# Row maxima of an attention in three bank fillings instead of four, with its stages dealt over six slots instead of seven

## The chip, the cores and the metric

The kernel is one program on one core of a Trainium2 chip. The metric is the device time of one execution in microseconds (us). The core has TensorE (PE in the profile, its weight loads PEld), VectorE (DVE), ScalarE (ACT), GpSimd (POOL) and SyncE (SP), which here only issues transfers. Each takes its own instructions in program order; they meet through semaphores. TensorE writes PSUM, eight banks of 128 partitions by 512 fp32 numbers, and VectorE and ScalarE read it out.

## The reference

Two transformer-like layers over x, 8 batches of 112 rows of 256, with a context of 8 batches of 375 rows. The first step is the one that the change touches:

```
x = x + attention_16_heads(layernorm(x), ctx, ctx)     # heads of 16 columns, scores 112 x 375 a head
x = x + mixture_of_8_experts(layernorm(x))             # each token to its best expert, 112 a slot
x = x + attention_1_head(layernorm(x), ctx, ctx, mask)
x = x + ffn_with_low_rank(layernorm(x))

scores = einsum(q, k) / sqrt(16); attn = softmax(scores, over the 375)
out = (attn @ v) @ Wo.T + bo
```

The softmax of the first attention takes each row's true maximum over the 375 context rows off before the exponential.

## The kernel before

The first attention works block by block; a block is a batch of 112 rows with its 16 heads. The heads stand in four groups of four. A head of a group lies on its own 32 partitions, so four matmuls of 32 rows run side by side into banks 0 to 3, one bank a head. Banks 0 and 1 are the LOW pair and 2 and 3 the HIGH pair: each pair has one semaphore for filled and one for drained, and both kinds of filling below share them. `open_tiles` waits until the pair's last filling is read out.

- Row maxima, `row_max(b, g)`: queries times keys, 112 rows by 375 columns for the four heads of group g, four fillings a block (M0 to M3 in the text below). VectorE reduces each pair of banks with one instruction of 2x375 columns and writes the negative maximum to `mneg`.
- Scores, `scores(b, step)`: keys times queries, context rows on the partitions, three fillings a block (S0 to S2). Each has two parts of 224 columns; the negative maxima are added by a small bf16 matmul (L461) ahead of the fp32 one (L466). ScalarE takes the exponential of each pair (L870).
- `weighted(b, step)`: exponentials times values (L484), into bank 4, for all three steps together, 96 instructions. Only in block 7 it comes step by step.

An fp32 matmul appears in the trace as two instructions of the same line, one behind the other.

A block's work is dealt over slots. `steps()` runs i from -1 to 9 and a slot u from 0 to SLOTS-1. In slot u of step i stand: a scores filling of block i where `SCORE_AT` says so, a row maximum of block i+1 where `MAX_AT` says so, the weighting of block i, and then the small stages of `PIPE[u]`, each with the number of blocks that it is behind (-1 is the next block, -2 the one after). All engines walk the same table, so it sets the order of every queue. The stages are:

- K0, K1: keys (L384), copied by ScalarE (L832). V0 to V2: values (L412), copied by L853. QX, Q0, Q1: transposed x and queries of two blocks.
- ND0, ND1: VectorE splits the maxima of two groups into two bf16 pieces; NM0, NM1: TensorE transposes them (L529), ScalarE copies (L899).
- U: ScalarE copies bank 4. C1: TensorE turns it, VectorE divides. C2, C3: turned back and multiplied by Wo (L553), x added, moments. L2: layer norm. C4: transposed x (L375). C5: logits of the experts (L565), read by VectorE, then an Exp on ScalarE that waits for VectorE. D5, C6, D6: the choice of expert, running counts (L575), indices, and GpSimd's scatter of the rows.

Small stages take the banks 5, 6 and 7 in turn. In step 0 and before it VectorE also has the first norms of later batches (`FIRST_NORMS`). Where blocks run out, TensorE is given projections of the second attention's values (L507, 24 chunks of 125x256): `CTX_AT` and `CTX_FILL` place some in the first attention's last steps, `CTX_BEFORE_EXPERTS` ahead of the experts, the remainder behind them. The experts (L607, L617) wait for the scattered rows, which SyncE loads from DRAM as soon as the last scatter has landed.

Of the kernel before, what the change touches and what calls it, by code (L numbers as in the profile page):

```python
# [31 lines left out]
SLOTS = 7  # L32
SCORE_STEPS = 3
SCORE_AT = {0: 0, 2: 1, 4: 2}
MAX_AT = {1: 0, 3: 1, 5: 2, 6: 3}
# [8 lines left out]
    0: [("NM1", 0), ("C1", 1), ("D5", 2), ("V0", -1)],  # L44
    1: [("C2", 1), ("C6", 2), ("K0", -2), ("D6", 2)],
    2: [("C3", 1)],
    3: [("V1", -1)],
    4: [("L2", 1), ("ND0", -1), ("K1", -2)],
    5: [],
    6: [("U", 0), ("NM0", -1), ("C4", 1), ("V2", -1), ("C5", 1), ("ND1", -1)],  # L50
# [4 lines left out]
Q_SLOTS = {(0, 2): "QX", (0, 3): "Q0", (1, 2): "Q1"}  # L55
# [28 lines left out]
CTX_AT = {(6, 1): 1, (6, 4): 1, (7, 0): 1, (7, 4): 2}  # L84
CTX_BEFORE_EXPERTS = 7
# [21 lines left out]
def extras(i, u):  # L107
    for stage, behind in PIPE[u]:
        first = FIRST_K if stage[0] == "K" else 0
        if first <= i - behind < NB:  # L110
            yield stage, i - behind
    if (i % 2, u) in Q_SLOTS and i >= 0 and i // 2 + 1 < QCHUNKS:
        yield Q_SLOTS[i % 2, u], i // 2 + 1
# [36 lines left out]
def build(nc, A):  # L150
    out = A["out"]
    with ExitStack() as ctx:
# [67 lines left out]
        mneg = sb("mneg", [S, 2, H])  # L220
        mpieces = sb("mpieces", [S, DT, 2, P], BF16)
# [129 lines left out]
        def _(pe):  # L351
# [86 lines left out]
            def row_max(b, g):  # L438

                m, a = divmod(g, 2)  # L440
                read(("K", b, m))
                read(("Q", b // 2, m))
                for half, pair in HALVES:
                    open_tiles(("MX", b, g), half)
                    for j in pair:
                        rows = slice(32 * j, 32 * j + 32)
                        mm = pe.matmul(bank(j)[0:S, 0:S2], qz[rows, m, a, b * S:(b + 1) * S], kt[b % 3][rows, m, :],  # L447
                                       start=True, stop=True)
                    mm.then_inc(filled[half], 1)
# [588 lines left out]
        def _(v):  # L1038
# [53 lines left out]
            def row_max(b, g):  # L1092
                for half, pair in HALVES:
                    _, free = full(("MX", b, g, half))
                    v.tensor_reduce(mneg[:, b % 2, PAIRS * g + pair.start:PAIRS * g + pair.stop],  # L1095
                                    ps[0:S, pair.start:pair.stop, 0:S2], AX.X, ALU.max, negate=True).then_inc(free, 1)

            def post(stage, b):
                if stage in ("ND0", "ND1"):

                    m = int(stage[2])
                    for half, _ in HALVES:
                        drained_by_me(("MX", b, 2 * m + 1, half))
# [465 lines left out]
```

## Time and profile before

| | |
|---|---|
| median of 3 runs | 375.06 us (374.88 to 376.21) |
| profiled execution | 374.57 us |
| its span in the trace | 372.8 us |
| PE busy in the span | 354.9 us, 95% |
| PEld, DVE, ACT, POOL busy | 268.6, 184.0, 151.5, 57.6 us |
| reduces of the row maxima, L1095 | 64, 57.1 us |
| granted TensorE clock, mean | 0.99 |

Busy time of an engine is the union of its records. A matmul's record starts when it is issued and its end is modelled, so TensorE's spacing is read from start to start of successive groups. A row of the timeline merges neighbours of one line; behind `<-` in brackets stands what ended the engine's idle time.

### The profile page before, as it was taken

How to read it: one execution, taken by the hardware profiler on the slowest of the kernel's cores; microseconds unless marked ns; L12 is line 12 of the kernel's file. 1: busy time of each engine (PE TensorE's matmuls, PEld its weight loads, DVE VectorE, ACT ScalarE, POOL GpSimd, SP SyncE). 2: the span in 40 equal slices, each digit the busy share in tenths (PEclk: the TensorE clock that was granted, in tenths of full speed). 3: DMA queues.
4: the chain of work that ended last, by engine and by line, in shares of the span. 5: the costliest groups of instructions: out<-in, count | busy, mean ns of one | idle time of the engine just before them, and what ended most of it. 6: DMA issues, size and time to landing. Idle time of an engine off the chain costs nothing.

```text
span 372.8 us, 7965 instructions
## 1 busy us (share of the span) xinstructions
PE 354.9 (95%) x3128; PEld 268.6 (72%) x3128; DVE 184.0 (49%) x573; ACT 151.5 (41%) x358; POOL 57.6 (15%) x95
## 2 busy tenths in 40 slices
PE   7969999999999999998989999999889999999996
PEld 6535566666576756566768998998768889797875
DVE  4764644756566584745461121212599677531500
ACT  2415463555546454535524221120345666423300
POOL 3220400010101010101020000030685321200000
PEclk9989999999999999999989999999999999999999
DMA  8936060610000010016108399960110011111000
GB/s 237 348 123 225 3 226 3 205 36 2 12 4 12 4 40 4 12 20 222 58 26 263 89 339 328 327 177 25 49 51 0 3 55 51 50 30 50 26 25 26
DMA packets 24886, 35.29 MB, mean 95 GB/s; under 512 B 2609, under 2 KB 21409, under 8 KB 24737
## 3 DMA queue, kind: packets, MB, share of 16 engines
q1 hardware_dynamic: 22160, 31.73, 26.1%
q0 software_dynamic: 768, 1.84, 1.7%
q10 hardware_dynamic: 1920, 1.21, 1.2%
q8 instruction: 25, 0.41, 0.4%
q14 instruction: 13, 0.10, 0.1%
HBM read 31.06 MB, written 3.72 MB: 93 GB/s over the span
## 4 chain that ended last, share of the span: by engine, by line
PE 49%; DVE 3%; ACT 2%; issue 1%; DMA 1%; POOL 0%; DVEq 0%; ACTq 0%; POOLq 0%; SPq 0%
PE ps L607 8%; PE ps L752 8%; PE ps L617 7%; PE ps L730 7%; PE ps L507 4%; PE ps L683 3%; PE ps L699 2%; PE ps L673 2%; PE ps L375 1%; PE ps L484 1%; PE ps L743 1%; PE ps L760 1%; PE ps L466 1%; DMA xn<-expert_out_dram,idx_get 1%; ACT heads L870 1%
## 5 line engine op out<-in xcount | busy, mean ns | idle before, releaser
L1095 DVE TENSOR_REDUCE mneg<-ps 112x2 f32<-112x750 f32 x64 | 57.1, 933 | 43.4 <-PE ps L447 43.2
L447 PE MATMUL ps<-heads 32*112 32x375 f32 x256 | 39.3, 519 | 3.6 <-DVE mneg L1095 2.9
L870 ACT ACTIVATE heads<-ps 125x896 f32<-125x896 f32 x34 | 29.3, 915 | 12.7 <-PE ps L466 12.7
L1310 POOL TENSOR_TENSOR rstd<-veps,neghalf 112x1 f32<-112x1 f32 x32 | 18.6, 581 | 78.0 <-DVE veps L1059 77.8
L607 PEld LDWEIGHTS ps<-xT,ring 128*128 128x128 f32 x256 | 29.8, 192 | 1.2 <-ACT xT L823 0.7
L607 PE MATMUL ps<-xT,ring 128*128 128x112 f32 x256 | 29.9, 275 | 0.5 <-ACT xT L823 0.5
L752 PE MATMUL ps<-heads,ring 128*112 128x256 f32 x128 | 28.8, 382 | 0.0
L447 PEld LDWEIGHTS ps<-heads 32*112 32x112 f32 x256 | 14.9, 170 | 19.3 <-issue 13.9
L617 PE MATMUL ps<-ring,heads 128*112 128x256 f32 x128 | 28.8, 379 | 0.0
L466 PE MATMUL ps<-heads 32*125 32x224 f32 x384 | 27.2, 363 | 0.0
L412 PE MATMUL ps<-w_in,ctxT 128*125 128x256 f32 x96 | 26.8, 403 | 0.0
L752 PEld LDWEIGHTS ps<-heads,ring 128*112 128x112 f32 x128 | 22.4, 177 | 6.1 <-issue 1.4
L1355 POOL DMA_INDIRECT expert_in_dram<-xn,idx_put x8 | 8.0, 1000 | 115.9 <-DVE idx_put L1159 115.9
L617 PEld LDWEIGHTS ps<-ring,heads 128*112 128x112 f32 x128 | 22.1, 177 | 4.4
L507 PE MATMUL ps<-w_in,ctxT 128*125 128x256 f32 x96 | 25.1, 404 | 0.0
L730 PE MATMUL ps<-xT,heads 128*128 128x224 f32 x128 | 24.9, 353 | 0.0
L384 PE MATMUL ps<-ctxT,w_in 128*128 128x375 f32 x64 | 24.1, 499 | 0.0
L730 PEld LDWEIGHTS ps<-xT,heads 128*128 128x128 f32 x128 | 24.0, 190 | 0.1
L1198 DVE TENSOR_SCALAR heads<-ps,b1col 128x112 f32<-128x112 f32 x32 | 8.6, 328 | 30.8 <-PE ps L607 30.7
L933 ACT ACTIVATE heads<-ps,b1col 128x112 f32<-128x112 f32 x32 | 8.7, 354 | 33.1 <-PE ps L607 33.1
L1003 ACT ACTIVATE ring<-ring,fb1col 128x224 f32<-128x224 f32 x32 | 13.6, 474 | 19.0 <-DVEq L1255 18.9
L412 PEld LDWEIGHTS ps<-w_in,ctxT 128*125 128x125 f32 x96 | 16.6, 194 | 6.1 <-issue 4.3
(149 smaller groups left out, 567.7 us busy)
## 6 DMA issues: line engine op xcount, KB each, us to landing
ring<-in_L_ffn_W SPq DMA_DIRECT2D x16, 1024.0 KB, 6.3
ctxT<-in_ctxT SPq DMA_DIRECT2D x8, 375.0 KB, 11.2
heads<-in_L_ffn_W SPq DMA_DIRECT2D x2, 1024.0 KB, 9.7
ring<-x_by_odd_rows_dram SPq DMA_DIRECT2D x4, 448.0 KB, 3.6
ring<-in_mask SPq DMA_DIRECT2D x1, 1312.5 KB, 7.0
expert_in_dram<-eo SPq DMA_DIRECT2D x1, 896.0 KB, 10.8
b2row<-in_L_ffn_b SPq DMA_DIRECT2D x8, 112.0 KB, 7.2
out_dram<-ring SPq DMA_DIRECT2D x8, 112.0 KB, 1.9
```

The lines of the kernel that those rows point to most:

```text
L384: mm = pe.matmul(o[:, 0:S2], w_in[:, 1, k, m * P:(m + 1) * P], ctxT[:, k, b * S2:(b + 1) * S2], start=k == 0, stop=k == DT - 1)
L412: mm = pe.matmul(o[0:KC, 0:D], ctxT[:, k, b * S2 + c * KC:b * S2 + (c + 1) * KC], w_in[:, 2, k, :], start=k == 0, stop=k == DT - 1)
L447: mm = pe.matmul(bank(j)[0:S, 0:S2], qz[rows, m, a, b * S:(b + 1) * S], kt[b % 3][rows, m, :], start=True, stop=True)
L466: mm = pe.matmul(bank(j)[0:KC, x * QW:(x + 1) * QW].rearrange("p (a q) -> p a q", a=2), kt[b % 3][rows, m, c * KC:(c + 1) * KC], qz[rows, ...
L507: mm = pe.matmul(o[0:KC, 0:D], ctxT[:, k, b * S2 + c * KC:b * S2 + (c + 1) * KC], wv_at1[:, k, :], start=k == 0, stop=k == DT - 1)
L607: mm = pe.matmul(o[:, f * S:(f + 1) * S], w1e[e % RING][:, k, ft * P:(ft + 1) * P], xT[:, k, e * S:(e + 1) * S], start=k == 0, stop=k == D ...
L617: mm = pe.matmul(o[0:S, 0:D], hid[e % 2][:, ft, :], w2e[e % RING][:, ft, :], start=ft == 0, stop=ft == FT - 1)
L730: mm = pe.matmul(o[:, f * 2 * S:(f + 1) * 2 * S], w1f[:, k, ft * P:(ft + 1) * P], xT[:, k, 2 * p * S:2 * (p + 1) * S], start=k == 0, stop= ...
L752: pe.matmul(o[0:S, 0:D], gT[p % 2][:, ft, x * S:(x + 1) * S], w2f[:, ft, :], start=ft == 0, stop=False)
L870: act.activation(weights(b, step)[0:KC, pair.start:pair.stop, :], ps[0:KC, pair.start:pair.stop, 0:2 * QW], ACT.Exp, scale=DK ** -0.5).the ...
L1095: v.tensor_reduce(mneg[:, b % 2, PAIRS * g + pair.start:PAIRS * g + pair.stop], ps[0:S, pair.start:pair.stop, 0:S2], AX.X, ALU.max, negate ...
L1310: g.tensor_tensor(rstd[:, b:b + 1], veps[:, b:b + 1], neghalf[:, b:b + 1], ALU.pow)\
```

## The change

Row maxima are taken in three fillings a block. Group 0 and group 3 each have their 375 columns in a filling of their own (the first and the third), and the remaining 125 columns of those banks take a third of group 1 and of group 2. The second filling has 250 columns of group 1 and 250 of group 2. VectorE reduces the second filling with one instruction a pair that gives both groups; of the first and the third it reduces the 125 columns into `mpart` and the 375 into `mneg`, and ND0 and ND1 begin with the minimum of `mneg` and `mpart`, a new instruction. A half is reported filled behind the second part.

There are six slots. The logits (C5) move from the slot of C4 to slot 1 two steps behind, counts and indices (C6, D6) from slot 1 to slot 3, the choice D5 from slot 0 to slot 2. Queries of two blocks are made in an order that starts with a transposition an iteration earlier. Some values stages stand a slot or a step earlier for the first blocks. Six, not seven projections stand ahead of the experts and two more in the steps 6 and 7. SyncE loads the second attention's value weights behind Q0 of the last pair, not Q1.

```diff
--- before.py
+++ after.py
@@ -29,10 +29,13 @@
 
 
 
-SLOTS = 7
+SLOTS = 6
 SCORE_STEPS = 3
 SCORE_AT = {0: 0, 2: 1, 4: 2}
-MAX_AT = {1: 0, 3: 1, 5: 2, 6: 3}
+MAX_AT = {1: 0, 3: 1, 5: 2}
+MAX_PARTS = (((0, 0, 375), (1, 0, 125)), ((1, 125, 375), (2, 0, 250)), ((3, 0, 375), (2, 250, 375)))
 
 
 WEIGHTED_AT = {5: (0, 1, 2)}
@@ -41,18 +44,21 @@
 HALVES = ((LOW, range(0, 2)), (HIGH, range(2, 4)))
 
 PIPE = {
-    0: [("NM1", 0), ("C1", 1), ("D5", 2), ("V0", -1)],
-    1: [("C2", 1), ("C6", 2), ("K0", -2), ("D6", 2)],
-    2: [("C3", 1)],
-    3: [("V1", -1)],
-    4: [("L2", 1), ("ND0", -1), ("K1", -2)],
-    5: [],
-    6: [("U", 0), ("NM0", -1), ("C4", 1), ("V2", -1), ("C5", 1), ("ND1", -1)],
+    0: [("NM1", 0), ("C1", 1), ("V0", -1)],
+    1: [("C2", 1), ("C5", 2), ("K0", -2)],
+    2: [("D5", 2), ("C3", 1)],
+    3: [("L2", 1), ("ND0", -1), ("K1", -2), ("V1", -1), ("C6", 2), ("D6", 2)],
+    4: [("V2", -1), ("C4", 1), ("NM0", -1)],
+    5: [("U", 0), ("ND1", -1)],
 }
 FIRST_K = 1
 
 QW, QCHUNKS, FIRST_Q = 2 * S, NB // 2, 1
-Q_SLOTS = {(0, 2): "QX", (0, 3): "Q0", (1, 2): "Q1"}
+Q_SLOTS = {(0, 2): "Q1", (0, 4): "Q0", (1, 2): "QX"}
+EARLY = {(-1, 2): [("V1", 0)], (-1, 5): [("QX", 1), ("V0", 1)]}
+MOVED = {(-1, 3): [("V1", 0)], (0, 0): [("V0", 1)]}
 
 
 
@@ -81,8 +87,8 @@
 
 
 CTX_FILL = {"C2": 1, "C3": 1, "C4": 2, "C6": 1}
-CTX_AT = {(6, 1): 1, (6, 4): 1, (7, 0): 1, (7, 4): 2}
-CTX_BEFORE_EXPERTS = 7
+CTX_AT = {(6, 1): 2, (6, 3): 1, (7, 0): 1, (7, 2): 1, (7, 4): 2}
+CTX_BEFORE_EXPERTS = 6
 CTX_AFTER_FIRST_UP = 1
 CTX_BEHIND_FOLD = 1
 CTX_IN_SECOND = {0: 1, 1: 1}
@@ -107,10 +113,11 @@
 def extras(i, u):
     for stage, behind in PIPE[u]:
         first = FIRST_K if stage[0] == "K" else 0
-        if first <= i - behind < NB:
+        if first <= i - behind < NB and (stage, i - behind) not in MOVED.get((i, u), ()):
             yield stage, i - behind
-    if (i % 2, u) in Q_SLOTS and i >= 0 and i // 2 + 1 < QCHUNKS:
-        yield Q_SLOTS[i % 2, u], i // 2 + 1
+    yield from EARLY.get((i, u), ())
+    if (i % 2, u) in Q_SLOTS and i >= 0 and (i + 3) // 2 < QCHUNKS:
+        yield Q_SLOTS[i % 2, u], (i + 3) // 2
 
 
 def weighted_in(i, u):
@@ -218,6 +225,7 @@
         cc = sb("cc", [S, D])
         ccT = sb("ccT", [P, DT, S])
         mneg = sb("mneg", [S, 2, H])
+        mpart = sb("mpart", [S, 2, PAIRS])
         mpieces = sb("mpieces", [S, DT, 2, P], BF16)
         maxT = sb("maxT", [P, DT, 2 * S], BF16)
         onesc = sb("onesc", [P, KC], BF16)
@@ -435,18 +443,23 @@
             pe.wait_ge(ld["wv"], 16)
 
 
-            def row_max(b, g):
-                m, a = divmod(g, 2)
-                read(("K", b, m))
-                read(("Q", b // 2, m))
-                for half, pair in HALVES:
-                    open_tiles(("MX", b, g), half)
-                    for j in pair:
-                        rows = slice(32 * j, 32 * j + 32)
-                        mm = pe.matmul(bank(j)[0:S, 0:S2], qz[rows, m, a, b * S:(b + 1) * S], kt[b % 3][rows, m, :],
-                                       start=True, stop=True)
-                    mm.then_inc(filled[half], 1)
+            def row_max(b, step):
+                for g, _, _ in MAX_PARTS[step]:
+                    read(("K", b, g // 2))
+                    read(("Q", b // 2, g // 2))
+                for n, (g, lo, hi) in enumerate(MAX_PARTS[step]):
+                    m, a = divmod(g, 2)
+                    at = n * (MAX_PARTS[step][0][2] - MAX_PARTS[step][0][1])
+                    for half, pair in HALVES:
+                        if n == 0:
+                            open_tiles(("MX", b, step), half)
+                        for j in pair:
+                            rows = slice(32 * j, 32 * j + 32)
+                            mm = pe.matmul(bank(j)[0:S, at:at + hi - lo], qz[rows, m, a, b * S:(b + 1) * S],
+                                           kt[b % 3][rows, m, lo:hi], start=True, stop=True)
+                        if n == 1:
+                            mm.then_inc(filled[half], 1)
 
             def scores(b, step):
 
@@ -1089,18 +1102,27 @@
             v.wait_ge(ld_x[1], 16)
 
 
-            def row_max(b, g):
+            def row_max(b, step):
                 for half, pair in HALVES:
-                    _, free = full(("MX", b, g, half))
-                    v.tensor_reduce(mneg[:, b % 2, PAIRS * g + pair.start:PAIRS * g + pair.stop],
-                                    ps[0:S, pair.start:pair.stop, 0:S2], AX.X, ALU.max, negate=True).then_inc(free, 1)
+                    _, free = full(("MX", b, step, half))
+                    js = slice(pair.start, pair.stop)
+                    if step == 1:
+                        top = mneg[:, b % 2, PAIRS:3 * PAIRS].rearrange("p (g j) -> p j g", j=PAIRS)[:, js, :]
+                        v.tensor_reduce(top, ps[0:S, js, 0:500].rearrange("p j (g k) -> p j g k", g=2), AX.X, ALU.max,
+                                        negate=True).then_inc(free, 1)
+                    else:
+                        top = mneg[:, b % 2, PAIRS * MAX_PARTS[step][0][0]:][:, js]
+                        v.tensor_reduce(mpart[:, step // 2, js], ps[0:S, js, 375:500], AX.X, ALU.max, negate=True)
+                        v.tensor_reduce(top, ps[0:S, js, 0:375], AX.X, ALU.max, negate=True).then_inc(free, 1)
 
             def post(stage, b):
                 if stage in ("ND0", "ND1"):
 
                     m = int(stage[2])
                     for half, _ in HALVES:
-                        drained_by_me(("MX", b, 2 * m + 1, half))
+                        drained_by_me(("MX", b, m + 1, half))
+                    split = mneg[:, b % 2, PAIRS * (m + 1):PAIRS * (m + 2)]
+                    step(v.tensor_tensor(split, split, mpart[:, m, :], ALU.min))
                     if b:
                         v.wait_ge(*filled_at(("NM", b - 1, m)))
                     top = mneg[:, b % 2, 2 * PAIRS * m:2 * PAIRS * (m + 1)].rearrange("p (a j) -> p a j", a=2)
@@ -1442,7 +1464,7 @@
             for e in range(RING - 1):
                 wait_filled(("ST", e, 0, HIGH))
                 load_expert(e)
-            wait_filled(("Q", QCHUNKS - 1, DT - 1))
+            wait_filled(("Q", QCHUNKS - 1, 0))
             sp.dma_start(wv_at1, kp_of("L1_xattn_Wv")).then_inc(ld_wv_at1, 16)
 
             sp.wait_ge(pv_units, SCORE_STEPS * (NB - 1))
```

On TensorE, from the row maximum in slot 1 of step 3 to the stage behind S1. Before:

```order
L447 MATMUL ps<-heads 112x375 x4
L544 MATMUL ps<-ident,cc 128x112 x2
L575 MATMUL ps<-onehot,tri 112x8
L576 MATMUL ps<-seen,onesb 112x8
L384 MATMUL ps<-ctxT,w_in 128x375 x2
L461 MATMUL ps<-maxT,onesc 125x224 x4
L466 MATMUL ps<-heads 125x224 x4
L461 MATMUL ps<-maxT,onesc 125x224 x4
L466 MATMUL ps<-heads 125x224 x4
L553 MATMUL ps<-w_in,ccT 112x256 x2
```

And now:

```order
L459 MATMUL ps<-heads 112x375 x4
L459 MATMUL ps<-heads 112x125 x4
L557 MATMUL ps<-ident,cc 128x112 x2
L578 MATMUL ps<-wg,xT 112x8 x2
L392 MATMUL ps<-ctxT,w_in 128x375 x2
L474 MATMUL ps<-maxT,onesc 125x224 x4
L479 MATMUL ps<-heads 125x224 x4
L474 MATMUL ps<-maxT,onesc 125x224 x4
L479 MATMUL ps<-heads 125x224 x4
L566 MATMUL ps<-w_in,ccT 112x256 x2
```

The row maximum has its second part of 125 columns, the logits (L578) stand ahead of the keys (L392), and the counts have gone from here.

On TensorE, the end of step 2: the keys, the last row maxima around the weighting (L484), and what comes behind it. Before:

```order
L384 MATMUL ps<-ctxT,w_in 128x375 x2
L447 MATMUL ps<-heads 112x375 x4
L484 MATMUL ps<-heads,vones 17x112 x32
L484 MATMUL ps<-ring,vones 17x112 x16
L447 MATMUL ps<-heads 112x375 x4
L529 MATMUL ps<-identb,mpieces 128x112 x2
L375 MATMUL ps<-ident,xn 128x112 x2
L412 MATMUL ps<-w_in,ctxT 125x256 x2
L565 MATMUL ps<-wg,xT 112x8 x2
```

And now, from the values ahead of the last row maximum to the scores of the next block:

```order
L420 MATMUL ps<-w_in,ctxT 125x256 x2
L383 MATMUL ps<-ident,xn 128x112 x2
L542 MATMUL ps<-identb,mpieces 128x112 x2
L412 MATMUL ps<-xT,w_in 128x224 x2
L459 MATMUL ps<-heads 112x375 x4
L459 MATMUL ps<-heads 112x125 x4
L497 MATMUL ps<-heads,vones 17x112 x32
L497 MATMUL ps<-ring,vones 17x112 x16
L474 MATMUL ps<-maxT,onesc 125x224 x4
```

The weighting stood between M2 and M3; now it stands between the last row maximum and the next block's scores, and the transposed x and the maxima of NM0 are ahead of it.

On ScalarE, around slot 1. L905 and L918 are the Exp of the logits, L832 and L845 the keys' copy, L870 and L883 the exponentials of the scores. Before:

```order
L853 ACTIVATE vones<-ps 125x16x16
L905 ACTIVATE ex,small<-lg,small 112x8
L870 ACTIVATE heads<-ps 125x896 x2
L899 ACTIVATE maxT<-ps 128x224
L853 ACTIVATE vones<-ps 125x16x16
L891 ACTIVATE ccT<-ps,bcol 128x112 x2
L832 ACTIVATE heads<-ps,bcol 128x375
L870 ACTIVATE heads<-ps 125x896 x2
```

And now:

```order
L883 ACTIVATE heads<-ps 125x896 x2
L912 ACTIVATE maxT<-ps 128x224
L866 ACTIVATE vones<-ps 125x16x16
L904 ACTIVATE ccT<-ps,bcol 128x112 x2
L918 ACTIVATE ex,small<-lg,small 112x8
L845 ACTIVATE heads<-ps,bcol 128x375
L883 ACTIVATE heads<-ps 125x896 x2
```

The logits' Exp stood right ahead of S0's exponentials; it now stands ahead of the keys' copy and S1's.

## Rows read from the trace of the kernel before

**Rows 1.** Stretches: us, busy us of each engine (instructions), PEclk, DMA share, GB/s.
```profile
41.30:163.06 121.76, 119.46 (x1475) 78.02 (x1473) 71.91 (x205) 62.55 (x123) 9.61 (x13) 1.00 0.13 43
163.06:198.96 35.90, 32.49 (x387) 24.99 (x386) 17.99 (x77) 15.48 (x38) 4.06 (x5) 0.95 0.31 101
```

**Rows 2.** Timeline, PE, a block: start us, us, line, out<-in, xcount, idle before.
```profile
61.52 1.74 PE L484 MATMUL ps<-heads,vones 125*17 125x112 f32 x64
...
63.95 0.90 PE L447 MATMUL ps<-heads 32*112 32x375 f32 x8
64.79 0.27 PE L529 MATMUL ps<-identb,mpieces 112*128 112x112 bf16 x2
...
65.10 1.04 PE L412 MATMUL ps<-w_in,ctxT 128*125 128x256 f32 x4
65.98 0.47 PE L565 MATMUL ps<-wg,xT 128*112 128x8 f32 x4
...
67.85 0.27 PE L529 MATMUL ps<-identb,mpieces 112*128 112x112 bf16 x2
...
69.36 1.28 PE L447 MATMUL ps<-heads 32*112 32x375 f32 x8
70.57 0.41 PE L544 MATMUL ps<-ident,cc 112*128 112x112 f32 x2
...
72.34 0.32 PE L461 MATMUL ps<-maxT,onesc 2*125 2x224 bf16 x4
...
73.46 1.12 PE L553 MATMUL ps<-w_in,ccT 128*112 128x256 f32 x4
...
74.89 1.41 PE L447 MATMUL ps<-heads 32*112 32x375 f32 x8
76.23 1.13 PE L412 MATMUL ps<-w_in,ctxT 128*125 128x256 f32 x4
77.19 0.92 PE L404 MATMUL ps<-xT,w_in 128*128 128x224 f32 x4
78.05 0.32 PE L461 MATMUL ps<-maxT,onesc 2*125 2x224 bf16 x4
78.19 0.56 PE L466 MATMUL ps<-heads 32*125 32x224 f32 x8
78.59 0.26 PE L461 MATMUL ps<-maxT,onesc 2*125 2x224 bf16 x4
...
79.17 1.53 PE L384 MATMUL ps<-ctxT,w_in 128*128 128x375 f32 x4
80.63 1.38 PE L447 MATMUL ps<-heads 32*112 32x375 f32 x8
```

**Rows 3.** Timeline of the same block, other engines and weight loads.
```profile
64.89 1.78 DVE L1095 TENSOR_REDUCE mneg<-ps 112x2 f32<-112x750 f32 x2 [1.85 <-PE ps L447]
...
66.73 0.13 PEld L461 LDWEIGHTS ps<-maxT,onesc 2*125 2x125 bf16 x2 [0.22 <-DVE mneg L1095]
...
67.17 0.30 ACT L905 ACTIVATE ex<-lg,small 112x8 f32<-112x8 f32 x1 [0.61 <-DVE small L1139]
...
67.98 1.73 ACT L870 ACTIVATE heads<-ps 125x896 f32<-125x896 f32 x2 [0.41 <-PE ps L466]
...
72.32 0.16 DVE L1155 TENSOR_REDUCE small<-tmp 112x1 f32<-112x8 f32 x1
...
72.50 0.57 ACT L832 ACTIVATE heads<-ps,bcol 128x375 f32<-128x375 f32 x1 [0.89 <-PE ps L384]
...
75.41 0.27 PEld L447 LDWEIGHTS ps<-heads 32*112 32x112 f32 x4 [0.25 <-ACT heads L870]
```

**Rows 4.** Timeline at 30 and at 195 us; DMA issues from 195 us.
```profile
30.35 0.90 PE L384 MATMUL ps<-ctxT,w_in 128*128 128x375 f32 x2
...
195.58 0.80 SPq L1459 DMA_DIRECT2D xn<-expert_in_dram  x2
...
xn<-expert_in_dram SPq DMA_DIRECT2D x2, 112.0 KB, 2.1
```

## The prediction

> **What bounds the kernel now.** I read the windows first, one over six blocks of the first attention and one for its tail. From 41.30 to 163.06 TensorE's records cover 119.46 of 121.76 us, 20.3 a block, while VectorE has 71.9 and ScalarE 62.6 [rows 1]. That looks like a TensorE bound, but a record of a matmul also covers its wait for tiles, so I went to the timeline of one block and took TensorE's spacing, start to start [rows 2]. I call a scores filling S0 to S2, a row maximum filling M0 to M3, the low pair of banks LOW and the high pair HIGH.
>
> The fillings that meet free tiles give the bare prices. M3 takes 0.84 (63.95 to 64.79), S1 takes 1.12 (72.34 to 73.46). M0 and M1 are the same eight instructions and take 1.21 (69.36 to 70.57) and 1.34 (74.89 to 76.23). What holds them stands in [rows 3]: ScalarE's two exponentials start 0.13 behind the end of S0 (67.85) and last 1.73, and the weight load for HIGH at 75.41 waits for such a one. From the end of a scores filling to the end of the next row maximum it is 2.72 (S0 to M0) and 2.77 (S1 to M1), whatever the 1.51 and 1.43 us of work between are: 1.95 until HIGH is free and 0.82 for the HIGH half alone. The reduces do the same to S0: they start 0.10 behind the end of M3, last 1.78, HIGH is free at 66.73, and S0 ends 1.12 later, 3.06 behind M3. Bare work would be 2.35, 2.27 and 2.71 (0.31+0.88+0.40+1.12) for these three stretches. S2 to M2 is like S1 to M1, so 1.7 of 20.3 us goes in handing over the four banks. A block hands them over seven times.
>
> **The change part by part.** I go by six stretches of a block, each from the end of one filling to the end of the next.
>
> *The filling of 500 columns.* A row maximum now has two parts a tile, 375+125, 250+250 and 375+125 columns. The columns of a block stay; there are 48 instructions for 32. Two passes of 224 columns of a scores filling start 0.40 apart from the next group (78.19 to 78.59), 0.20 a pass, 0.89 ns a column. A pass of 125 is 0.11, one of 250 is 0.22. So 375+125 costs 0.84+0.22=1.06, and 250+250 costs 0.17 (0.84 less two passes of 0.335)+0.88=1.05. The cheapest reading is that the second part hides beside the HIGH half of the first (0.95); the dearest is that each pass keeps M3's 0.42 per 375 columns, 0.09 over its columns: 1.24. I take 1.05, because two passes in a row are what the scores rows show. Three fillings are 3.15 against 3.36 for four bare ones.
>
> Here a rule speaks against the change. The 0.09 over the columns of M3 shows that a weight load is not always hidden [rows 2]. The Trainium skill (TensorE: Matmul & The Clock Gate, Part 3, what overlaps and what doesn't) says that a weight load overlaps running matmuls only where its row group differs. Both passes and both parts use the same row group, so by it all four loads are exposed. The scores rows, at 0.20 for 224 columns, do not bear it out fully.
>
> *The reduces.* Two of 750 elements a row last 1.78, 0.89 each, and a reduce of 8 elements 0.16 [rows 3]. That is 0.98 ns an element over a fixed 0.15. One of 250 is then 0.40 and one of 1000 is 1.14. M0 and M2 need 2x(0.89+0.40)=2.6, or 2.5 where starts overlap; M1 needs 2.3; both instead of 1.78. Over a block that is 7.3 against 7.12, with two small minima at some 0.2 each; VectorE has 8 us idle. But each handover is longer by up to 0.8, and that lies between a row maximum and the next scores. LOW is complete only when its second part is, 0.6 to 1.0 behind HIGH's release, HIGH about 0.2 later. With M's end 1.05 behind release, HIGH is free 2.0 to 2.4 behind M's end. I take 2.2. If the reduces overlap nothing and wait for the whole filling it is 2.9; if LOW's second part runs far ahead it is 1.8.
>
> *The slots, now with the work that each stretch holds* [rows 2]:
> S0 to M0: first context turn and values, 1.51, bare 2.56. The exponentials set it: 1.95+1.05=3.00.
> M0 to S1: 1.77 (second context turn, counts, keys) and the logits with 0.40 (its record has 0.47), 2.17; with S 3.29. The reduces ask 2.2+1.12=3.32. I take 3.35.
> S1 to M1: 3.00. The logits' Exp stands ahead of the keys' copy on ScalarE. It started 0.50 behind the reduces' end (66.67 to 67.17), so now it comes 2.7 behind M0; with 0.4 and the copy's 0.57 ScalarE is free at 3.7, where S1's exponentials could start at 3.48. Bounds 0 and 0.3 (0.3 if M0's reduces end late); queued behind it are those exponentials, and M1's HIGH half waits for them. I take 0.05, as VectorE could also be done at 2.0.
> M1 to S2: keys 1.46 (79.17 to 80.63), values 0.96 (76.23 to 77.19), counts under 0.1, S 1.12: 3.6. The reduces need 3.2, hidden.
> S2 to M2: values 0.88, two transposes 0.31 (64.79 to 65.10), in even blocks queries 0.86 (77.19 to 78.05): 3.1; in odd ones the exponentials' 3.00.
> M2 to next S0: weighting 2.43 (61.52 to 63.95) covers the reduces; with S 3.55.
> Sum 19.65 even, 19.55 odd. In block 6 projections of the second attention stand in for keys, one more than before: 3.0+3.7+3.0+3.1+3.0+3.55=19.35. Blocks 1 to 6 are 117.3 in sum. Before they are 121.8: block 1's S0 ends at 41.30+2.43+0.84+3.06=47.6, block 7's at 163.06 plus the same 6.33, 169.4. This saves **4.5**, of which 1.0 is the projection drawn in and the rest fewer and partly fuller handovers.
>
> *Opening.* Block 0's row maxima are chained through VectorE before and after, with norms of two batches among them; I leave the end of M0 for block 1 at 30.35 [rows 4]. From there 3.4+3.0+3.5+3.0+3.55=16.4 against 17.3 before: **0.9** saved. Bounds: +1.5 (queries and values moved ahead wait) and -2.
>
> *Tail.* From block 7's S0 to its counts the chain goes through three exponentials with nothing to reduce, then C1 to C4 and the norm's steps. Logits and counts now come an iteration later, but both then stand behind the same norm, so I take it at no change (up to 0.5 later if VectorE is still at block 6's indices). Then six projections for seven stand ahead of the experts. The rows for expert 0 were asked for at 195.58 and took 2.1 [rows 4], so they are there at 197.7, 1.2 ahead of the transposes at 198.96. One projection, 0.96, fits in that: **0.9** saved. Behind the experts one projection fewer lies beside the gather, nothing. SyncE's wait on the other query half frees the value weights' load a little earlier, nothing.
>
> Sum: 0.9+4.5+0.9=6.3. The profiled run took 374.57 (span 372.8, 1.8 around it), so 368.3; the median of before is 0.5 higher, 368.8. I say **368.5**.
>
> **The rivals.**
> A, weight loads exposed: M at 1.24 adds 0.19 to three stretches, 0.57 a block, 3.4 in six: 371.7. For it speaks M3's own 0.42 a pass, against it the scores' 0.20. This is what the rule of the skill above gives here.
> B, slower: the drain becomes the bound. Place: M0 to S1 and M2 to S0. HIGH free 2.9 behind M's end makes both 4.0, ScalarE's held Exp adds 0.3 to S1 to M1: 3.0+4.0+3.3+3.65+3.1+4.0=21.05 against 20.3, +0.75 in six blocks, +1 in block 0, less 0.9: 379. It decides from where two such stretches sum to 7.6, that is HIGH free 2.7 behind M. For it: reduces are the longest single thing between fillings. Against it: the 2.43 of weighting lies over one of the two.
> C, the clock: the tail's window had 0.95 of the clock, so 3.6 us of its 35.9 at 1.2 GHz [rows 1], after TensorE had waited in short pieces. One more stretch like that (behind the experts, where a projection is missing, or in the opening) costs up to 1.7: 370; one fewer gives 366.8.
> D, it does not do what it says: handovers are 6 for 7, but the time comes back as waits elsewhere (a copy held on ScalarE, norms in block 0), each stretch near 3.4: 20.3 a block, 374.
>
> **How the numbers follow.** Forecast 0.50 (own range 366.5 to 370.5), A 0.18, C 0.12, D 0.11, B 0.09. The range goes from C's good side less 1 to D: 365.5 to 374. No change means within 0.5% of 375.06 (373.2 to 376.9), about what a measurement tells apart. Faster: all of the forecast, A and C less 0.02, 0.78; same: D and a little of A and B, 0.14; slower: 0.08.
>
> **What would show it.** In the changed profile: blocks of 19.5 to 19.7 from weighting to weighting; row maximum groups 1.03 to 1.08 behind HIGH's release (1.24 is A); the small reduces at 0.40, and HIGH free 2.2 behind M (2.9 is B); S0 of block 7 ending near 164; experts near 192.6. I am wrong if a block is over 20, or if exponentials of S1 start over 0.3 behind the scores.

## The result, and the profile after

The changed kernel takes 371.69 us (median of 6, 371.33 to 373.43) against 374.97 (6, 374.28 to 376.21): a ratio of 0.9919, interval 0.9892 to 0.9946. It is faster, by 3.3 us; 6.5 were predicted. The profiled execution took 372.57 us with a span of 370.8, 2.0 less than before; for it the sum gave 368.3. Half of the gain is missing, and I look for it stretch by stretch. In three of the runs below (V2 by VectorE, norms later, values not early) one execution is slow (376.54, 376.12 and 376.50 us, clock 0.973 to 0.977); it is in their medians and ranges but not in their ratios, and the first one's profile is of it.

The same stretches as [rows 1], from the first block's weighting to the last one's and on to the experts, and then the opening up to the end of block 1's S0, after and before:

```profile
45.31:165.25 119.94, 116.95 (x1574) 84.09 (x1570) 75.51 (x228) 60.92 (x124) 9.88 (x14) 1.00 0.14 44
165.25:197.34 32.09, 28.53 (x371) 22.19 (x369) 17.85 (x78) 14.83 (x36) 4.03 (x5) 1.00 0.30 102
```

```profile
0.00:49.03 49.03, 42.70 (x386) 29.12 (x387) 27.72 (x74) 18.23 (x34) 12.76 (x31) 0.90 0.59 178
```

```profile
0.00:47.63 47.63, 41.63 (x350) 26.10 (x351) 26.99 (x66) 17.31 (x32) 12.71 (x31) 0.96 0.59 183
```

I cut at the ends of S0, as the prediction did:

| stretch | predicted | measured |
|---|---|---|
| opening, to the end of block 1's S0 | -0.9 | 47.63 to 49.03: +1.4 |
| six blocks, to the end of block 7's S0 (168.87) | -4.5 | 121.77 to 119.84: -1.9 |
| from there to the experts | -0.9 | 29.56 to 28.47: -1.1 |
| experts and all behind them | 0 | 173.84 to 173.46: -0.4 |

The blocks end at 49.03, 68.50, 89.49, 109.02, 130.02, 149.54 and 168.87. Odd blocks take 19.5, block 6 takes 19.3, but blocks 2 and 4 take 21.0. TensorE through block 2, the answer to [rows 2], preceded by the last stretch of block 1 in the first two lines:

```profile
61.90 1.13 PE L420 MATMUL ps<-w_in,ctxT 128*125 128x256 f32 x4
...
64.88 1.74 PE L497 MATMUL ps<-heads,vones 125*17 125x112 f32 x64
...
68.50 0.27 PE L542 MATMUL ps<-identb,mpieces 112*128 112x112 bf16 x2
...
70.00 1.50 PE L459 MATMUL ps<-heads 32*112 32x375 f32 x16
71.43 0.41 PE L557 MATMUL ps<-ident,cc 112*128 112x112 f32 x2
71.68 0.47 PE L578 MATMUL ps<-wg,xT 128*112 128x8 f32 x4
...
73.44 0.72 PE L474 MATMUL ps<-maxT,onesc 2*125 2x224 bf16 x4
...
74.98 1.12 PE L566 MATMUL ps<-w_in,ccT 128*112 128x256 f32 x4
...
76.78 1.21 PE L459 MATMUL ps<-heads 32*112 32x250 f32 x16
77.92 1.53 PE L392 MATMUL ps<-ctxT,w_in 128*128 128x375 f32 x4
...
81.42 1.13 PE L420 MATMUL ps<-w_in,ctxT 128*125 128x256 f32 x4
82.39 0.36 PE L383 MATMUL ps<-ident,xn 112*128 112x112 f32 x2
82.58 0.26 PE L542 MATMUL ps<-identb,mpieces 112*128 112x112 bf16 x2
83.74 0.99 PE L412 MATMUL ps<-xT,w_in 128*128 128x224 f32 x4 [0.90 <-ACT vones L866]
84.67 1.11 PE L459 MATMUL ps<-heads 32*112 32x375 f32 x16
85.71 1.74 PE L497 MATMUL ps<-heads,vones 125*17 125x112 f32 x64
...
88.38 0.69 PE L479 MATMUL ps<-heads 32*125 32x224 f32 x8
...
89.49 0.27 PE L542 MATMUL ps<-identb,mpieces 112*128 112x112 bf16 x2
```

S0 to M0 is 2.93 (68.50 to 71.43), M0 to S1 3.55, S1 to M1 2.94, M1 to S2 3.50. S2 to M2 is 2.98 in the odd block (61.90 to 64.88) and 4.29 in the even one (81.42 to 85.71); the wait of 0.90 ahead of the queries (L412) is in the even one alone. A filling of two parts that meets free banks takes 1.04 (M2, 84.67 to 85.71); M1, whose HIGH pair comes free 0.06 behind its start, takes 1.14. Behind the release of HIGH, M0 ends 1.08 later (70.35 to 71.43) and M1 too (76.84 to 77.92). M2 to S0 is 3.62 in the odd block (64.88 to 68.50), 3.78 in the even one.

VectorE, ScalarE and the weight loads of the same block, the answer to [rows 3]:

```profile
68.62 1.73 ACT L883 ACTIVATE heads<-ps 125x896 f32<-125x896 f32 x2 [0.62 <-PE ps L479]
...
71.37 0.42 DVE L1115 TENSOR_REDUCE mpart<-ps 112x2 f32<-112x250 f32 x1 [1.33 <-PE ps L459]
71.70 0.93 DVE L1116 TENSOR_REDUCE mneg<-ps 112x2 f32<-112x750 f32 x1
...
72.55 0.41 DVE L1115 TENSOR_REDUCE mpart<-ps 112x2 f32<-112x250 f32 x1
72.87 0.93 DVE L1116 TENSOR_REDUCE mneg<-ps 112x2 f32<-112x750 f32 x1
...
73.86 0.13 PEld L474 LDWEIGHTS ps<-maxT,onesc 2*125 2x125 bf16 x2 [0.28 <-DVE mneg L1116]
...
74.31 0.30 ACT L918 ACTIVATE ex<-lg,small 112x8 f32<-112x8 f32 x1 [1.83 <-DVE small L1161]
...
75.11 1.73 ACT L883 ACTIVATE heads<-ps 125x896 f32<-125x896 f32 x2
...
81.59 1.73 ACT L883 ACTIVATE ring<-ps 125x896 f32<-125x896 f32 x2 [0.87 <-PE ps L479]
...
83.21 0.39 ACT L866 ACTIVATE vones<-ps 125x256 f32<-125x256 f32 x1
```

The four reduces behind M0 stand one behind the other, 71.37 to 73.80, and HIGH is free 2.43 behind M0's end (73.86). The logits' Exp (74.31) delays nothing: S1's exponentials start 0.13 behind the scores. The last two rows are the cause of the wait. Small stages take the banks 5, 6, 7 in turn. Behind S2 come V2 (81.42), the transposed x, NM0, and in even blocks the queries as a fourth, which take V2's bank again. ScalarE copies V2 only behind S2's two exponentials, at 83.21, and with its 0.39 the bank comes free at 83.6.

The opening and the rows for the experts, the answer to [rows 4]:

```profile
24.36 0.31 PE L474 MATMUL ps<-maxT,onesc 2*125 2x224 bf16 x2 [1.72 <-DVE mneg L1116]
25.43 0.45 PE L474 MATMUL ps<-maxT,onesc 2*125 2x224 bf16 x2 [0.77 <-DVE mneg L1116]
...
28.62 1.77 PE L459 MATMUL ps<-heads 32*112 32x375 f32 x7 [0.71 <-ACT heads L883]
...
195.25 1.27 SPq L1481 DMA_DIRECT2D xn<-expert_in_dram  x3
...
197.34 0.41 PE L383 MATMUL ps<-ident,xn 112*128 112x112 f32 x2 [0.93 <-DMA xn<-expert_in_dram]
```

Block 0's S0 waits 1.72 and 0.77 us for VectorE, which has the norms of batches 4 and 5 ahead of M2's reduces; 0.71 for ScalarE follows. From 25.35 on the granted clock is at half (1.2 GHz) for 10.24 us; before, one such stretch of 3.41 lies in the opening, and another of 3.41 begins at 190.95. That makes the opening's 0.90 against 0.96.

### The profile page after: what moved, and what is told of

Same layout as the page of the kernel before. It is cut to its first block, busy times and chain, and to the rows that moved or that the text cites. A ratio compares the mean times of both kernels' runs of the same rounds, so it can differ in the third digit from the quotient of the medians.

```text
span 370.8 us, 8282 instructions
## 1 busy us (share of the span) xinstructions
PE 350.9 (95%) x3256; PEld 275.1 (74%) x3256; DVE 188.6 (51%) x605; ACT 150.1 (40%) x358; POOL 57.8 (16%) x95
## 4 chain that ended last, share of the span: by engine, by line
PE 80%; DVE 8%; DMA 4%; issue 3%; ACT 2%; POOL 1%; ACTq 0%; DVEq 0%; POOLq 0%; SPq 0%
PE ps L459 9%; PE ps L620 8%; PE ps L765 8%; PE ps L630 7%; PE ps L743 7%; PE ps L479 5%; PE ps L497 5%; PE ps L420 5%; PE ps L392 4%; DVE mneg L1116 3%; PE ps L474 3%; PE ps L696 2%; PE ps L520 2%; PE ps L566 2%; PE ps L712 2%
## 5 line engine op out<-in xcount | busy, mean ns | idle before, releaser
L459 PE MATMUL ps<-heads 32*112 32x375 f32 (+2 forms) x384 | 36.3, 404 | 1.2 <-ACT heads L883 0.9
L883 ACT ACTIVATE heads<-ps 125x896 f32<-125x896 f32 x34 | 29.3, 915 | 14.1 <-PE ps L479 14.1
L459 PEld LDWEIGHTS ps<-heads 32*112 32x112 f32 x384 | 21.9, 175 | 15.4 <-issue 6.3
L1116 DVE TENSOR_REDUCE mneg<-ps 112x2 f32<-112x750 f32 x32 | 29.7, 928 | 0.0
L1115 DVE TENSOR_REDUCE mpart<-ps 112x2 f32<-112x250 f32 x32 | 13.2, 412 | 31.1 <-PE ps L459 31.1
L479 PE MATMUL ps<-heads 32*125 32x224 f32 x384 | 28.2, 373 | 0.0
L420 PE MATMUL ps<-w_in,ctxT 128*125 128x256 f32 x96 | 25.6, 389 | 0.0
L392 PE MATMUL ps<-ctxT,w_in 128*128 128x375 f32 x64 | 25.5, 523 | 0.0
L520 PE MATMUL ps<-w_in,ctxT 128*125 128x256 f32 x96 | 23.8, 385 | 0.0
L1111 DVE TENSOR_REDUCE mneg<-ps 112x4 f32<-112x1000 f32 x16 | 18.5, 1196 | 7.7 <-PE ps L459 7.7
```

Source lines behind the costliest of these rows:

```text
L392: mm = pe.matmul(o[:, 0:S2], w_in[:, 1, k, m * P:(m + 1) * P], ctxT[:, k, b * S2:(b + 1) * S2], start=k == 0, stop=k == DT - 1)
L420: mm = pe.matmul(o[0:KC, 0:D], ctxT[:, k, b * S2 + c * KC:b * S2 + (c + 1) * KC], w_in[:, 2, k, :], start=k == 0, stop=k == DT - 1)
L459: mm = pe.matmul(bank(j)[0:S, at:at + hi - lo], qz[rows, m, a, b * S:(b + 1) * S], kt[b % 3][rows, m, lo:hi], start=True, stop=True)
L479: mm = pe.matmul(bank(j)[0:KC, x * QW:(x + 1) * QW].rearrange("p (a q) -> p a q", a=2), kt[b % 3][rows, m, c * KC:(c + 1) * KC], qz[rows, ...
L520: mm = pe.matmul(o[0:KC, 0:D], ctxT[:, k, b * S2 + c * KC:b * S2 + (c + 1) * KC], wv_at1[:, k, :], start=k == 0, stop=k == DT - 1)
L883: act.activation(weights(b, step)[0:KC, pair.start:pair.stop, :], ps[0:KC, pair.start:pair.stop, 0:2 * QW], ACT.Exp, scale=DK ** -0.5).the ...
```

## The experiments

Each is timed against the kernel before on the same chip. There were three groups on three chips: the kernel before stood at 375.37 beside the first four runs, at 374.93 beside the next four and at 374.66 beside the last three. Ends of block 1's S0 are from the profiled execution of each.

**V2 copied by VectorE in the even blocks.** It empties V2's bank without ScalarE's exponentials.

```diff
+def by_dve(stage, b):
+    return stage == "V2" and b in (3, 5)
...
-                    copy_v(b, int(stage[1]))
+                    if not by_dve(stage, b):
+                        copy_v(b, int(stage[1]))
...
+                elif stage == "V2":
+                    o, free = full(("V", b, 2))
+                    v.tensor_copy(vones[b % 2][0:KC, 2, :, 0:DK],
+                                  o[0:KC, 0:D].rearrange("p (h w) -> p h w", h=H)).then_inc(free, 1)
```

> The changed kernel, with one copy moved: in the two blocks (2 and 4) that have a query stage Q0 behind V2, C4 and NM0 the values of V2 are copied out of PSUM by VectorE instead of ScalarE. Theory (three small banks): Q0 is the fourth small filling since S2 and waits for V2's bank, which ScalarE frees only behind S2's exponentials; then the stretch S2 to M2 falls from 4.28 us to 3.2 to 3.3 us in both blocks and the kernel gets 2.0 us faster. Rival (ScalarE simply has too much to do in even blocks): the wait comes back at the next stretch, under 0.7 us in all. Rival (nothing to do with the bank): 4.28 stays, time unchanged.

Measured 372.06 (370.51 to 376.54), ratio 0.9894 (0.9872 to 0.9916). In its block 2:

```profile
80.62 1.13 PE L424 MATMUL ps<-w_in,ctxT 128*125 128x256 f32 x4
...
81.89 0.42 DVE L1159 COPY vones<-ps 125x256 f32<-125x256 f32 x1 [0.15 <-PE ps L424]
...
82.46 0.99 PE L416 MATMUL ps<-xT,w_in 128*128 128x224 f32 x4 [0.41 <-DVE vones L1159]
```

S2 to M2 falls from 4.29 to 3.81 in both even blocks: the bank is the cause, since only who empties it has changed. The time doesn't come back in the next stretch, M2 to S0, which is 3.71 for 3.78. But I expected 3.2 to 3.3. V2 is full only 1.27 behind its start (80.62 to 81.89), and its bank free 0.42 later; the two small stages between it and the queries are done by then, so TensorE still waits 0.41. The median shows no difference from the changed kernel; 1.0 us was at stake and its runs spread by more.

**Norms of batches 4 and 5 from slot 4 of step -1 to slot 0 of step 0.**

```diff
-FIRST_NORMS = {(-1, 0): (2, 3), (-1, 4): (4, 5), (0, 4): (6, 7)}
+FIRST_NORMS = {(-1, 0): (2, 3), (0, 0): (4, 5), (0, 4): (6, 7)}
```

> The changed kernel, with the norms of batches 4 and 5 moved on VectorE from slot 4 of step -1 to slot 0 of step 0. Theory (opening bound by VectorE): the last row maxima's reduces start at 21.1 instead of 22.96, S0 of block 0 ends 2 us earlier or more, and TensorE's clock is not halved or shorter; block 1's S0 ends 2 to 4 us earlier than 49.0, the kernel is 2 to 3 us faster. Rival (norms are only moved): VectorE makes them ahead of the next row maximum's reduces and the stretch M0 to S1 of block 0 gets longer by as much; under 0.7 us.

Measured 370.08 (369.38 to 376.12), ratio 0.9865 (0.9845 to 0.9886). The wait of 1.72 is gone, that of 0.77 stays, and one stretch of 3.41 at half is left. Block 1's S0 ends at 45.80, 3.2 us earlier, which holds both the wait and two half stretches fewer. Against the kernel before on its chip the run is 5.3 us faster, 2.0 more than the changed kernel is. The timeline's row of the wait that stays, and the opening's window:

```profile
24.47 0.31 PE L474 MATMUL ps<-maxT,onesc 2*125 2x224 bf16 x2 [0.77 <-DVE mneg L1116]
```

```profile
0.00:45.80 45.80, 41.10 (x386) 28.52 (x387) 27.79 (x74) 18.09 (x34) 12.73 (x31) 0.96 0.64 191
```

**Nine more matmuls ahead of block 0's S0,** into the next small bank, so that TensorE isn't idle there. Everything else is the changed kernel.

```diff
+                if b == 0 and step == 0:
+                    n = SPARE[(ring_bank[0] + 1) % 3]
+                    pe.wait_ge(drained[n], drains[n])
+                    for _ in range(9):
+                        pe.matmul(bank(n)[:, 0:P], ident[:, :], ident[:, :], start=True, stop=True)
```

> The changed kernel, with nine extra matmuls of 128x128 (2 us) ahead of block 0's first scores, where TensorE waits for VectorE. The wait for VectorE stays as it is. Theory (clock): the opening's half-clock stretch, 10.2 us in the profiled run of the changed kernel, goes or shrinks to 3.4 us; block 1's S0 ends near 47.0 instead of 49.0; median 0.7 to 2 us faster, since not every run had the long stretch. Rival (the loss in the opening is the waits alone): block 1's S0 stays at 49.0 and the time is unchanged.

Measured 371.85 (369.89 to 373.58), ratio 0.9907 (0.9877 to 0.9937). The opening and a stretch behind the experts:

```profile
0.00:46.48 46.48, 41.63 (x404) 29.68 (x405) 27.70 (x74) 18.21 (x34) 12.77 (x31) 1.00 0.62 188
257.00:268.00 11.00, 10.08 (x50) 8.22 (x49) 6.42 (x20) 2.98 (x11) 8.18 (x10) 0.69 0.19 54
```

At full clock the opening's end is 46.48, 2.55 less, though the norms still stand ahead of the reduces. The median doesn't follow, and the 0.7 to 2 us expected of it are missed: in this profile 6.83 us at half now lie at 259.6.

**Values of the first blocks in their usual slots** (only QX stays early):

```diff
-EARLY = {(-1, 2): [("V1", 0)], (-1, 5): [("QX", 1), ("V0", 1)]}
-MOVED = {(-1, 3): [("V1", 0)], (0, 0): [("V0", 1)]}
+EARLY = {(-1, 5): [("QX", 1)]}
+MOVED = {}
```

> The changed kernel without its special places for three values stages of the first blocks (V1 of block 0 back in slot 3, V0 of block 1 back in slot 0 of step 0). Theory: V0 of block 1 was lying in TensorE's wait for VectorE (22 to 24 us) for nothing, so without it the wait grows and 0.9 us of work comes behind S0, but there it lies beside exponentials: 0 to 0.7 us slower. Rival (they only shift work): unchanged; rival (they lengthened the idle stretch's loss): faster.

Measured 371.70 (370.69 to 376.50), ratio 0.9904 (0.9882 to 0.9927): no difference by time. Its opening ends at 47.01 with 3.41 us at half.

**Q0 behind the weighting,** one slot later.

```diff
-Q_SLOTS = {(0, 2): "Q1", (0, 4): "Q0", (1, 2): "QX"}
+Q_SLOTS = {(0, 2): "Q1", (0, 5): "Q0", (1, 2): "QX"}
```

> The changed kernel with the query stage Q0 of even blocks in slot 5, behind the weighting, instead of slot 4. Theory (three small banks, the copy of V2 behind S2's exponentials): with three small fillings between S2 and the last row maximum nothing waits, the stretch S2 to M2 of blocks 2 and 4 is 2.98 us instead of 4.28; M2 to S0 grows from 3.78 to 2.44+0.93+1.13=4.5. Net 0.6 us a block in two blocks and about nothing in block 0: 1.2 us faster than the changed kernel. Rival (even blocks are bound by ScalarE's work): the sum of both stretches stays 8.06.

Measured 372.00 (371.07 to 374.94), ratio 0.9934 (0.9912 to 0.9957). TensorE in its block 2:

```profile
81.79 1.13 PE L420 MATMUL ps<-w_in,ctxT 128*125 128x256 f32 x4
...
84.77 1.74 PE L497 MATMUL ps<-heads,vones 125*17 125x112 f32 x64
...
87.21 1.02 PE L412 MATMUL ps<-xT,w_in 128*128 128x224 f32 x4
...
89.30 0.27 PE L542 MATMUL ps<-identb,mpieces 112*128 112x112 bf16 x2
```

S2 to M2 is 2.98 (81.79 to 84.77), as in odd blocks: without a fourth filling the wait is gone. M2 to S0 grows from 3.78 to 4.53, since the queries' 0.96 no longer hides beside anything. Blocks 2 and 4 are 20.4, 0.56 shorter each; block 0 loses 0.7, as it had no such wait (no transposed x stands there yet). Net 0.4, under what the medians tell, where 1.2 were expected.

**One projection back in block 6.**

```diff
-CTX_AT = {(6, 1): 2, (6, 3): 1, (7, 0): 1, (7, 2): 1, (7, 4): 2}
+CTX_AT = {(6, 1): 1, (6, 3): 1, (7, 0): 1, (7, 2): 1, (7, 4): 2}
```

> The changed kernel with one projection fewer in slot 1 of step 6, which puts one more behind the experts, where before had it. Theory 1 (block 6 has no use for it): M0 to S1 of block 6 falls only from 3.60 to the reduces' 3.55, so nothing is gained there. Theory 2 (clock): with it TensorE waits 1.0 instead of 1.9 us at 265 us, and executions with a half-clock stretch there (one of 10.2 us was in the profile of e1) get rarer, the median is 0 to 0.8 us faster and its spread is smaller. Rival: the projection behind the experts costs its 0.96 us, slower by that.

Measured 371.93 (371.38 to 373.05), ratio 0.9924 (0.9900 to 0.9948). M0 to S1 of block 6 is 3.55 with one projection and 3.60 with two, and the block 19.23 and 19.33: the second lies beside the reduces almost whole. The median is where it was. From the experts to the end it is 173.6 (196.12 to 369.7) for 173.5, so the projection behind the experts costs some 0.1 and not its 0.96. Neither profile has a stretch at half behind the experts; one profile each doesn't tell whether the projection matters to the clock there.

**Norms, Q0 and projection together.**

```diff
+Q_SLOTS = {(0, 2): "Q1", (0, 5): "Q0", (1, 2): "QX"}
+FIRST_NORMS = {(-1, 0): (2, 3), (0, 0): (4, 5), (0, 4): (6, 7)}
+CTX_AT = {(6, 1): 1, (6, 3): 1, (7, 0): 1, (7, 2): 1, (7, 4): 2}
```

> The changed kernel with the norms of batches 4 and 5 later (as in e2), Q0 behind the weighting (as in e6) and one projection back behind the experts (as in e8). If the three causes are separate, their gains add: 1.6+1.2+0 to 0.8 us below the changed kernel's 371.7, so 368.0 to 369.2. If even blocks or the opening only shift their waits, 370 or more.

Measured 369.73 (368.52 to 370.00), ratio 0.9849 (0.9824 to 0.9874). The medians' 2.0 us below the changed kernel are about what the norms alone bring; block 0 pays for the late Q0, and this profile has 6.83 us at half in the opening. The expectation is missed by 0.5.

**Three fillings alone:** the changed row maxima with the seven slots and every place of the kernel before (PIPE, Q_SLOTS, CTX_AT, CTX_BEFORE_EXPERTS and SyncE's wait too).

```diff
-SLOTS = 6
+SLOTS = 7
...
-Q_SLOTS = {(0, 2): "Q1", (0, 4): "Q0", (1, 2): "QX"}
+Q_SLOTS = {(0, 2): "QX", (0, 3): "Q0", (1, 2): "Q1"}
...
+EARLY = {}
+MOVED = {}
```

> The first part of the change alone: row maxima in three fillings of 500 columns, with the seven slots and all places of stages, queries and projections of the kernel before. Theory (handovers by the longer reduces): stretches of a block 2.94, 3.5, 2.94, 3.4, 2.94 and M2 to S0 2.44+1.59+1.13=5.16, sum 20.9 us against 20.3 before, so 3 to 4 us slower than before. Rival (fewer handovers alone bring the gain): 19.8 a block, 3 us faster than before.

Measured 383.99 (382.74 to 387.00), ratio 1.0245 (1.0209 to 1.0281): 9 us slower, where 3 to 4 were expected. Even blocks take 21.0 (20.9 expected), and so does block 6; the odd ones take 22.6. Around M1 of an odd block:

```profile
56.35 1.73 ACT L884 ACTIVATE heads<-ps 125x896 f32<-125x896 f32 x2 [1.32 <-PE ps L480]
...
58.13 0.96 ACT L854 ACTIVATE heads<-ps,bq_par,parity 128x224 f32<-128x224 f32 x2
...
59.35 1.12 PE L460 MATMUL ps<-heads 32*112 32x250 f32 x16 [1.25 <-ACT heads L854]
```

The second filling takes groups 1 and 2, so it needs both halves of the queries, where four fillings needed the second half (Q1) only for M2. Q1's copy stands behind S1's exponentials, and M1 waits 1.25 for it. Three fillings in old places are no gain at all, not even in the blocks without this wait. The new places with four fillings were not tried, so what they are worth alone isn't shown.

**Norms later, and Q0 in slot 5 in blocks 2 and 4 only.**

```diff
+FIRST_NORMS = {(-1, 0): (2, 3), (0, 0): (4, 5), (0, 4): (6, 7)}
-    if (i % 2, u) in Q_SLOTS and i >= 0 and (i + 3) // 2 < QCHUNKS:
+    if (i % 2, u) in Q_SLOTS and i >= 0 and (i + 3) // 2 < QCHUNKS and not (i and u == 4):
         yield Q_SLOTS[i % 2, u], (i + 3) // 2
+    if i in (2, 4) and u == 5:
+        yield "Q0", (i + 3) // 2
```

> The changed kernel with the norms of batches 4 and 5 later (as in e2) and Q0 behind the weighting in blocks 2 and 4 alone; in block 0, where e6 lost 0.7 us by it, it stays in slot 4. Theory: e2's 370.1 less 2x0.56, 369.0. Rival (timed runs of these kernels differ only by their clock stretches now, e6's profile gained and its median did not): 370, no difference from e2.

Measured 369.98 (367.77 to 372.99), ratio 0.9888 (0.9848 to 0.9928). Block 1's S0 ends at 45.15, the six blocks take 118.82, 1.0 less than the changed kernel's. By time it can't be told from the run with the norms alone (370.08): 369.0 was expected, and what came is the rival's 370.

**The same with four more matmuls ahead of block 0's S0.**

```diff
+                if b == 0 and step == 0:
+                    n = SPARE[(ring_bank[0] + 1) % 3]
+                    pe.wait_ge(drained[n], drains[n])
+                    for _ in range(4):
+                        pe.matmul(bank(n)[:, 0:P], ident[:, :], ident[:, :], start=True, stop=True)
```

> As e11, with four extra matmuls of 128x128 (0.9 us) ahead of block 0's first scores, where TensorE waits for VectorE. Theory (clock): no half-clock stretch in the opening, block 1's S0 ends 0.9 us earlier per 3.4 us of stretch that is gone; 368.0 to 368.8. Rival (the stretch depends on where the window falls, not on these 0.9 us): as e11.

Measured 368.11 (366.93 to 370.77), ratio 0.9832 (0.9797 to 0.9868): better than both kernels, and as expected. Block 1's S0 ends 0.74 earlier than in the run before, which has 3.41 us at half in the opening; this one has none. The medians differ by 1.9, more than that explains, and their intervals overlap. Its opening and its stretch behind the experts:

```profile
0.00:44.41 44.41, 40.24 (x395) 28.82 (x395) 27.79 (x74) 18.11 (x34) 12.73 (x31) 1.00 0.63 197
254.00:266.00 12.00, 10.43 (x51) 8.41 (x51) 7.29 (x23) 3.36 (x12) 9.11 (x12) 0.72 0.17 49
```

**The kernel before with the norms later.**

```diff
-FIRST_NORMS = {(-1, 0): (2, 3), (-1, 4): (4, 5), (0, 4): (6, 7)}
+FIRST_NORMS = {(-1, 0): (2, 3), (0, 0): (4, 5), (0, 4): (6, 7)}
```

> The kernel before, with the norms of batches 4 and 5 moved on VectorE from slot 4 of step -1 to slot 0 of step 0, nothing else. Theory (the opening's wait is VectorE's norms in both kernels and no part of the change's effect): the wait of 2.9 us ahead of the last row maximum at 22.2 us goes, 2 to 3 us faster than before. Rival (only the changed kernel's longer reduces make VectorE late there): under 0.7 us.

Measured 371.76 (371.18 to 373.37), ratio 0.9937 (0.9917 to 0.9958). It is 2.9 us faster than the kernel before on its chip, within the 2 to 3 expected. In the kernel before, the last row maxima of block 0 wait 2.90 for the same norms (up to 22.24):

```profile
22.24 1.70 PE L447 MATMUL ps<-heads 32*112 32x375 f32 x8 [2.90 <-DVE mneg L1095]
```

And in this run, with its opening:

```profile
20.21 1.64 PE L447 MATMUL ps<-heads 32*112 32x375 f32 x8 [1.19 <-DVE mneg L1095]
```

```profile
0.00:44.14 44.14, 40.04 (x351) 25.59 (x351) 26.99 (x66) 17.24 (x32) 12.78 (x31) 1.00 0.65 198
```

The wait shrinks to 1.19, and block 1's S0 ends at 44.14, 3.5 earlier, with no stretch at half in the opening. The norms' place is a cost of both kernels. With it mended in both, they are 2.9 and 5.3 us faster than the kernel before on their chips: the change is then worth 2.4 us. The openings show none of it: at full clock they end at 44.14 here and at 44.41 in the changed kernel with four matmuls more.

## Why the prediction was wrong

The direction, the price of the fillings and most stretches were right; the size was off by 3.2 us, and in two blocks of six a wait came that the sum didn't have. The prediction's own sign of being wrong, a block over 20, came in both: 21.0.

*The filling and rival A.* 1.05 was predicted; 1.04 and 1.14 were measured, and 1.08 behind HIGH's release, not A's 1.24. The eight more instructions of M2 cost 0.20 over M3's 0.84, so the second part's passes do not pay the 0.09 over their columns again. By the Trainium skill (TensorE: Matmul & The Clock Gate, Part 3, what overlaps and what doesn't) a weight load overlaps running matmuls only in another row group; as all passes of a tile use one row group, they would pay it. These rows disagree, and they decide.

*The reduces and rival B.* The four behind M0 last 2.43 together and M1's two 2.31, where 2.5 to 2.6 and 2.3 were predicted. What was off is the head start of the LOW pair: its reduces begin only 0.06 ahead of M0's end (71.37). So HIGH is free 2.43 behind it, not 2.2, and M0 to S1 is 3.55 for 3.35. Behind the even blocks' M2, which meets free banks so that its LOW half does not run ahead, it is 2.67 (85.71 to 88.38), and M2 to S0 is 3.78 for 3.55. Both are within the bounds, and B's 2.9 doesn't come: B needed 2.7 in both stretches. Nor does the logits' Exp hold anything: S1 to M1 is 2.94.

*S2 to M2: the step that failed.* I summed the work of the even block ("values 0.88, two transposes 0.31 (64.79 to 65.10), in even blocks queries 0.86 (77.19 to 78.05): 3.1") and asked only whether the LOW and HIGH banks were free. The stretch now holds four small fillings, and there are three small banks. Measured 4.29 for 3.1, twice: 2.4 of the 2.5 us missing in the blocks (119.84 for 117.3). The remainder nets out: 0.3 to 0.4 over in the two stretches behind reduces together, 0.02 to 0.11 under in each of the others, so that odd blocks (19.5 for 19.55) and block 6 (19.33 for 19.35) are as predicted. The runs that let VectorE empty the bank (3.81) or take the fourth filling away (2.98) show it. This is rival D, "a copy held on ScalarE", in two blocks of six. That the fillings alone carry no gain, the run with them alone shows: even its 21.0 blocks are above the 20.3 of before. The gain needs the redealing.

*Opening.* Predicted 0.9 less, measured 1.4 more. The term was for the same clock. With nine matmuls added and no half stretch it ends at 46.48; with the values not early and as much at half as before (3.41) at 47.01, 0.6 less than before. The other 2.0 are, in the main, the 6.83 us more at half clock. That is rival C, which I had priced at up to 1.7 for one more stretch and given 0.12. How long the stretch is isn't a fixed property of the opening: two other runs whose opening is that of the changed kernel (the ones with V2 by VectorE and with one projection back) have 6.83 us and end at 48.23 and 48.05. Matmuls added ahead of block 0's S0, where TensorE waits, left no half stretch either time, which points to that wait; but of the five runs with the norms later one (all three together) still has 6.83 us. So why the stretch is three times as long in the changed kernel's profile as in the one before isn't settled. In the timed runs of both kernels the mean clock is mostly 0.99, so this term is larger in the profile (span 2.0 less) than in the medians (3.3 less).

*Tail.* The number, 0.9 for 1.1, came out for another reason. The rows were asked for 26.2 us behind block 7's S0 before and 26.4 after, and arrive 2.1 later: TensorE, a projection shorter, waits 0.93 for them. Before, 3.41 us at half lay there, worth some 0.85 by the estimate below; without it the projection would have brought only 0.2 to 0.3.

At equal clock the terms then are about 0.6+1.9+0.25+0.4=3.2, close to the difference of the medians; the 0.6 and the 0.25 are estimates.

*Behind the experts* 0.4 came that the sum had at nothing. The run with a projection put back there gives 0.1 of it; the remainder stays open.

## What to carry to other kernels

When stages are moved together, count the fillings of every bank ring between two points, not only the work: the fourth filling in a ring of three waits for the first one's reader, and it waits long if that reader stands behind a long instruction (0.90 us here, 0.41 with a free reader). When matrix products are packed into fewer fillings, look at which operands each now needs at once, and move their makers with them, or the saving turns into a wait (here 1.25 us in each odd block, in a version 9 us slower). In a stretch with short waits, price the clock at both levels before crediting anything under 1 us to the schedule.

## What the runs showed of the hardware

The half-clock stretches in these profiles last 3.41, 6.83 or 10.24 us. The opening of the changed kernel ends at 46.48 with none (nine matmuls added), 47.01 with 3.41 (values not early), 48.05 with 6.83 and 49.03 with 10.24. That is 0.85 us for each 3.41 on average, half of the 1.7 that a TensorE without waits would lose, and I take it as an estimate: TensorE waits for other engines during part of a stretch, and these openings also start up to 0.4 apart (their first transposed maxima, L542, stand at 19.90 to 20.28), so a single step says less. The changed kernel with norms later and Q0 moved ends its opening at 45.15 with 3.41, and with four matmuls more at 44.41 with none: 0.74. Over the fastest version's executions the spans go the same way, from 365.1 us at a mean clock of 1.00 to 369.0 at 0.98.

The stretches also move: profiles of six other versions, the one of before with later norms among them, have 3.41 to 10.24 us at half between 256 and 277 us, where their work differs from one of the two kernels by at most one projection and neither kernel's own profile has any. What brings them there stays open; executions of one kernel differ by it (0.98 to 1.00 in the mean clock, 366.9 to 370.8 us for the fastest version).
